# Attention and feed-forward in one kernel: the weighed values of a block accumulate in one PSUM bank, with V scaled by 16

## The reference, cut to what matters

```python
q = einsum('bsd,dhk->bshk', x, Wq) + bq          # k and v likewise
scores = einsum('bqhk,bshk->bhqs', q, k) / sqrt(K)
attn = softmax(scores, axis=-1)
ctx = einsum('bhqs,bshk->bqhk', attn, v)         # the change is here
attn_out = einsum('bqhk,hkd->bqd', ctx, Wo) + bo
```

## Time and profile before

| | |
|---|---|
| median of 3 executions | 3343.22 us (3339.74 to 3346.07) |
| the profiled execution | 3347.19 us, of which the span of the profile is 3345.4 us |
| PE busy | 3095.9 us, 93% of the span, 25440 matmuls |
| DVE busy | 2784.4 us, 83% |
| ACT busy | 2473.8 us, 74% |
| POOL busy | 2016.6 us, 60% |
| mean granted clock of PE | 0.969 of full speed |

### The profile page before, as it was taken

One profiled execution on the slowest core, in us unless ns is written; L12 is line 12 of the kernel. 1 busy time (PEld: TensorE's weight loads), 2 busy tenths in 40 slices (PEclk: granted clock), 3 DMA queues, 4 the chain that ended last, 5 costly groups with the idle time before them and its releaser, 6 DMA issues. The chain is left out here.

```text
span 3345.4 us, 77779 instructions
## 1 busy us (share of the span) xinstructions
PE 3095.9 (93%) x25440; PEld 2475.0 (74%) x25440; DVE 2784.4 (83%) x4983; ACT 2473.8 (74%) x4715; POOL 2016.6 (60%) x1550
## 2 busy tenths in 40 slices
PE   5899999999999999969999999999999999878897
PEld 4677777777777777757777777777777778667775
DVE  5688988888888888976888888888888889578886
ACT  3688888888888788856888787878888889733222
POOL 3577767676667666636777666766667677512232
PEclk9999999999999999989999999999999999989998
DMA  3522222222222122115122222222222222221110
GB/s 106 136 53 53 54 54 54 54 54 54 54 48 57 43 55 56 42 31 172 33 56 57 42 56 46 54 54 54 54 54 54 54 53 52 96 83 51 63 44 19
DMA packets 206585, 197.39 MB, mean 59 GB/s; under 512 B 157648, under 2 KB 180304, under 8 KB 193872
## 3 DMA queue, kind: packets, MB, share of 16 engines
q1 hardware_dynamic: 206160, 192.00, 24.7%
HBM read 53.16 MB, written 37.88 MB: 27 GB/s over the span
## 5 line engine op out<-in xcount | busy, mean ns | idle before, releaser
L442 POOL TENSOR_TENSOR p_l<-p_f,p_h 128x512 f16<-128x512 f32 x1280 | 1627.0, 1293 | 546.9 <-ACT p_h L514 546.1
L562 DVE TENSOR_REDUCE mx<-ps_aux 128x1 f32<-128x512 f32 x2048 | 1384.5, 684 | 289.3 <-PE ps_aux L735 258.8
L513 ACT ACTIVATE p_f<-ps_score 128x512 f32<-128x512 f32 x2048 | 1272.2, 622 | 358.7 <-PE ps_score L746 337.3
L514 ACT ACTIVATE p_h<-ps_score 128x512 f16<-128x512 f32 x2048 | 1283.0, 628 | 0.0
L735 PE MATMUL ps_aux<-k_hihi,q_hilo 128*128 128x512 f32 x2048 | 1037.5, 507 | 93.8 <-DVE mx L562 44.4
L768 PE MATMUL ps_ctx<-v_hi_one_lo,p_h 128*128 128x129 f16 x8192 | 929.2, 223 | 2.3 <-POOL p_l L442 1.5
L768 PEld LDWEIGHTS ps_ctx<-v_hi_one_lo,p_h 128*128 128x128 f16 x8192 | 609.2, 99 | 322.2 <-issue 264.2
L746 PE MATMUL ps_score<-q_hi_max,k_lo_one 65*128 65x512 f32 x2048 | 826.5, 404 | 0.0
L745 PE MATMUL ps_score<-q_hilo,k_hihi 128*128 128x512 f32 x2048 | 821.2, 401 | 3.7 <-DMA q_hi_max<-negm 3.1
L768 PE MATMUL ps_ctx<-v_hi_one_lo,p_l 128*128 128x65 f16 x8192 | 783.3, 195 | 0.0
L735 PEld LDWEIGHTS ps_aux<-k_hihi,q_hilo 128*128 128x128 f32 x2048 | 632.3, 309 | 173.1 <-DVE mx L562 69.1
(11 more groups left out here) (122 smaller groups left out, 2538.4 us busy)
## 6 DMA issues: line engine op xcount, KB each, us to landing
k_hihi<-hi_st SPq DMA_DIRECT2D x64, 512.0 KB, 8.6
v_heads<-v_new SPq DMA_DIRECT2D x64, 258.0 KB, 2.0
v_hi_one_lo<-v_heads SPq DMA_DIRECT2D x32, 516.0 KB, 9.7
q_hilo<-hi_st SPq DMA_DIRECT2D x32, 512.0 KB, 4.4
q_hilo<-lo_st SPq DMA_DIRECT2D x32, 512.0 KB, 6.6
q_hi_max<-hi_st SPq DMA_DIRECT2D x32, 512.0 KB, 9.2
k_lo_one<-lo_st SPq DMA_DIRECT2D x32, 512.0 KB, 10.1
heads<-ctx_n SPq DMA_DIRECT2D x128, 128.0 KB, 2.0
```

Source lines behind the costliest of these rows:

```text
L442: nc.gpsimd.tensor_tensor(p_l[:, r], p_f[:, r], p_h[:, r], ALU.subtract).then_inc(lo_pool, 1)
L513: nc.scalar.activation(p_f[:, r], ps_score[:, bank], ACT.Exp, scale=K ** -0.5)
L514: nc.scalar.activation(p_h[:, r], ps_score[:, bank], ACT.Exp, scale=K ** -0.5).then_inc(exp_done, 1)
L562: nc.vector.reduce_max(mx[:, blk % 2, tt, ch:ch + 1], ps_aux[:, bank], AX_X).then_inc(max_read, 1)
```

## The change

The context of a block accumulates in one bank: 4 x 65 columns instead of 4 x 129. For this the low part of V isn't scaled by 2048 any more; all of V is scaled by 16 instead (the column of ones holds 16 too), so the factor cancels in the division. `p_h` times the 64 low columns now goes onto the same 64 sums as `p_h` times the high ones, which takes a matmul of its own: 12 matmuls a step, of 65, 64 and 65 columns, where there were 8 of 129 and 65. The two banks hold two blocks in turn. ACT's copy and DVE's addition are gone. DVE takes the reciprocal and the product straight from the bank, both in step 4 of the next block. In the prologue DVE scales the bias of V once a batch, and the addition of that bias multiplies by 16 too.

```diff
-LO_SCALE = 2048.0
-SUMS_AT = 4
+V_SCALE = 16.0
+DIVIDE_AT = 4
...
-            def copy_sums(nb):
-
-                act.wait_ge(pv_done, (nb + 1) * KT + PROBS)
-                act.wait_ge(ev_step, nb * 2 + 2)
-                nc.scalar.activation(sums[:, :, :], ps_ctx[:, :, 0:2 * VW], ACT.Copy).then_inc(ctx_free, 1)
...
-                    nc.scalar.activation(v_new[:, k % 4, :, K + 1:VW], vf, ACT.Copy, scale=LO_SCALE)\
-                        .then_inc(v_ready, 1)
+                    nc.scalar.activation(v_new[:, k % 4, :, K + 1:VW], vf, ACT.Copy).then_inc(v_ready, 1)
...
-                    if t % KT == SUMS_AT and not (first and u == 0 and t < KT):
-                        copy_sums((g + u) * NB + t // KT - 1)
...
-            dve.sem_inc(ev_step, 2)
+            dve.sem_inc(ctx_free, 2)
...
-            def add_sums(nb):
-
-                dve.wait_ge(ctx_free, nb + 2)
-                acc = sums[:, :, :].rearrange("p a (t c) -> p (a t) c", c=VW)
-                nc.vector.scalar_tensor_tensor(out=ctx_u[:, :, :], in0=acc[:, :, K + 1:VW], scalar=1.0 / LO_SCALE,
-                                               in1=acc[:, :, 0:K], op0=ALU.mult, op1=ALU.add).then_inc(ev_step, 1)
+            def divide(j, nb):
+
+                acc = ps_ctx[:, j % 2, 0:TB * (K + 1)].rearrange("p (t c) -> p t c", c=K + 1)
+                dve.wait_ge(pv_done, (nb + 1) * KT + PROBS)
                 nc.vector.reciprocal(rden[:, :], acc[:, :, K]).then_inc(ev_step, 1)
-
-            def divide(j, nb):
-
-                dve.wait_ge(ev_step, nb * 2 + 4)
+                dve.wait_ge(ev_step, nb + 1)
                 dve.wait_ge(ctx_out[j % 2], (nb - j) * 8 + j // 2 * 16 + 16)
-                nc.vector.tensor_tensor(ctx_n[:, j % 2], ctx_u[:, :, :],
+                nc.vector.tensor_tensor(ctx_n[:, j % 2], acc[:, :, 0:K],
                                         rden[:, :].unsqueeze(2).to_broadcast([P, TB, K]), ALU.mult)\
-                    .then_inc(ctx_ready, 1)
+                    .then_inc(ctx_free, 1)
...
+                    nc.vector.tensor_scalar(bv_all, bv_all, V_SCALE, None, ALU.mult).then_inc(bv_scaled, 1)
+                    dve.wait_ge(bv_scaled, b + 1)
...
-                    if kt == 2 and block_before:
-                        add_sums((g + u) * NB + j - 1)
-                    if kt == 4 and block_before:
+                    if kt == DIVIDE_AT and block_before:
                         divide((j - 1) % NB, (g + u) * NB + j - 1)
...
                 for q in range(TB):
-                    acc = ps_ctx[:, q // 2, (q % 2) * VW:(q % 2 + 1) * VW]
-                    parts = [(p_h, VW), (p_l, K + 1)]
-                    if q % 2:
-                        parts.reverse()
-                    for p, width in parts:
-                        mm = nc.tensor.matmul(acc[:, 0:width], p[:, r, q * P:(q + 1) * P], V[u][:, kt, 0:width],
-                                              start=(kt == 0 and q % 2 == 0 and p is p_h),
-                                              stop=(kt == KT - 1 and q % 2 == 1 and p is p_h),
-                                              skip_group_check=True)
+                    acc = ps_ctx[:, j % 2, q * (K + 1):(q + 1) * (K + 1)]
+                    toks = slice(q * P, (q + 1) * P)
+                    v_one, v_lo = V[u][:, kt, 0:K + 1], V[u][:, kt, K + 1:VW]
+                    nc.tensor.matmul(acc, p_h[:, r, toks], v_one, start=(kt == 0 and q == 0), stop=False,
+                                     skip_group_check=True)
+                    nc.tensor.matmul(acc[:, 0:K], p_h[:, r, toks], v_lo, start=False, stop=False,
+                                     skip_group_check=True)
+                    mm = nc.tensor.matmul(acc, p_l[:, r, toks], v_one, start=False,
+                                          stop=(kt == KT - 1 and q == TB - 1), skip_group_check=True)
                 mm.then_inc(pv_done, 1)
```

More of the change, by code:

```diff
@@ L171, in attention @@
         negm = sb("negm", [P, 2, TB], F32R)
-        sums = sb("sums", [P, 2, 2 * VW], F32)
         rden = sb("rden", [P, TB], F32)
-        ctx_u = sb("ctx_u", [P, TB, K], F32)
         ctx_n = sb("ctx_n", [P, 2, TB, K], F32)
@@ L520, in head @@
                             .then_inc(xh_ready, 1)
-                    if t % KT == SUMS_AT and not (first and u == 0 and t < KT):
-                        copy_sums((g + u) * NB + t // KT - 1)
-                if last and u == 1:
-                    copy_sums((g + u) * NB + NB - 1)
                 return n
```

13 lines of the change are left out of this document (6 added, 7 removed).

## The result

The changed kernel takes 3384.27 us (median of 4, 3382.91 to 3385.39) against 3344.38 us of the kernel before: a ratio of 1.0122 (1.0109 to 1.0135), so 40 us or 1.2% slower. The forecast was 20 us slower, 3363 us in a range of 3315 to 3425. The profiled execution took 3384.6 us with a span of 3382.7 us, at the same mean granted clock as before, 0.969. So the 39.9 us are work or waits and not the clock.

A forecast was written before the change was run, and what follows sets the result against it. PE's own issue was taken as the bound within a head. Terms +29 (matmuls), +32 (burst end), -42 (DVE's relief) and +1 (ends) gave +20: 3367 us profiled, 3363 us median, with an 8-in-10 range of 3315 to 3425.

The forecast's parts named there:

- PE's two terms: PE's longer stream: the matmuls of a weigh, +29 us, and the end of the burst, +32 us.
- The matmuls of a weigh: PE, each quarter: three short matmuls at 30.5 ns, 91.5 ns against 88, over 8192 quarters: +29 us.
- the end of the burst: PE, last matmul of a burst: 65 columns hide 28 ns less of the next load, 1136 bursts: +32 us.
- The product from PSUM: DVE's product with its first operand in PSUM: 407 ns, its least, in place of a mean of 710.
- The waits that move: DVE's reciprocal now waits for the block's last weigh, with at least 2.3 us of slack: costed at nothing.
- ACT's copy: ACT loses 128 copies of 614 ns and 44.8 us of waiting; not the bound, so worth nothing.
- DVE's relief: DVE saves 1.08 us a block at best, cutting PE's waits for maxima: -42 us, bounds 0 and -55.
- The waits should fall from 44.4 to under 10: PE's waits of maximum tiles for DVE, in us, as a sign that would show the forecast.
- Short matmuls are dear: Rival: adding onto sums just written costs 5 ns more; 3429 us, or 3380 if half pay; set at 3405; chance 0.22.
- The relief wins: Rival: short matmuls at 29 ns or less, DVE gives back 50 us: -26, 3317 us; chance 0.28.
- point of decision: Where DVE's relief exceeds PE's two terms: a short matmul of 30.1 ns at 51 us of relief.
- The change doesn't do what it says: Rival: product from PSUM takes 0.7 us, PE gets back half: +21 more, 3384 us; within the dear side's 0.22.

The follow-up runs named there:

- the first experiment: Kernel before with the parts of a weigh never turned round, p_h first and p_l last, so bursts end with 65 columns: 3359.12 us, ratio 1.0044.

## Why the prediction was half right

The sign and PE's two terms held. The relief of DVE did not: its mechanism was wrong for this order of PE, and its term was nearly twice too large.

*The matmuls of a weigh, +29, and the end of the burst, +32.* Right, and a little low. A burst was to become 56 ns longer (8 quarters of 3.5 ns, and 28 at its end), 2.35 us for two steps; it became 62 ns longer, 2.362 us. That the sums agree so well, 61 forecast and 61.4 in the table, is partly luck: the table has 990 distances and the forecast more bursts. The short matmul was taken at 30.5 ns; from start to start it is 29, 33 and 29 ns in the median behind the three kinds, and 31.2 in the mean of a burst (718 ns in 23 distances). The end of the burst alone is 26 ns of the 28 forecast (the first experiment). That the load starts with the last matmul and takes 0.46 us whatever streams under it is what the earlier trace rows had said.

*The product from PSUM.* Right: 425 ns where 407 was forecast, with a spread of 3 ns where it had been 407 to 1316. "SBUF — State Buffer" of the Trainium skill, section "Who interferes with whom", says that one SBUF input keeps clear of GpSimd, and these numbers agree. The same trace has the other side of it in the subtractions with two SBUF inputs, at 1.54 and 1.24 us beside POOL's.

*The waits that move, and ACT's copy.* Right at nothing. The reciprocal waits for nobody in the timeline above, and for PE in 2 of 128 cases over the trace (4.8 us). ACT's 51 us show nowhere in PE's waits while PE's order is as it was; no run took ACT's copy away alone.

*DVE's relief, -42.* Wrong: the irregular distances gave back 23.6 us, of which 16.5 come with a longer PE stream alone, and the relief was -8 to -22 where it was measured by itself. This is the failing step, in its own sentence: "With 1.08 us less in that stretch most of the lag should be gone: 1.25 - 1.08, about 0.2 us, stay." The 1.08 us are about what was saved (0.78 of the addition, and 0.29 of the product by its mean). But I took DVE's lateness at `w_l` for a debt that runs through from the block's addition, and it isn't one. That "the next maxima run without a pause up to 672.71" was a misreading: DVE was ready and waiting for the tile at 664.88, behind the addition, so the addition's time was paid back before the lag began. In the trace after it stands idle for 0.97 us before 674.03 and is late again at 681.91. The lag is made in the 6 us behind that point, by two subtractions that run slowly beside POOL's, the cast and `w_l`. The earlier trace rows ended in just these, but the rows of the subtractions between 665.48 and 671.51 were left out of the reading, and so was the question that decides it, whether DVE is idle anywhere between the saved work and the late one. Of the saved work only the product's lies behind that point, 1.02 us that became 0.42; against it stand the reciprocal and the wait for it, 0.17 us each, so about 0.25 us is left (1.28 became 1.03), and from the next tile on it hardly shows. The experiments put it where it belongs: with the old order of PE no relief of the block touches the wait (28 times in each), and `w_l` off DVE removes it and is worth 38 to 43 us.

The same error sits in "The waits should fall from 44.4 to under 10": they fell to 36.2, and do so too with DVE untouched.

*The loop's turn.* Not in the sum: 33.6 to 39.4 us, +6. It is the same in the kernel with three matmuls and the old DVE work (39.6), and 34.9 and 32.1 us in the two kernels with eight matmuls a weigh (parts never reversed; DVE relieved), so it comes with PE's instructions. The page shows 4.90 MB of instructions in place of 3.82. That the fetch is what the turn waits for is an inference from these two rows, and no run took it apart.

Those 6 us are among the distances over 0.8 us, whose total falls by 1.7 in spite of them. Put right, the sum for the spans is 61 - 24 - 1 + 1 = 37, with the turn inside the 24; by the medians it is 40.

*The rivals.* "Short matmuls are dear" is out by its price: the same burst with and without a second matmul on the same sums takes 718 and 720 ns. It had stood at 3380 to 3429 us and the time fell into that stretch for another reason, a relief that was not there. A time in the range of a case is no proof of the case. "The relief wins" had its point of decision right (a short matmul of 30.1 ns with 51 us of relief), and missed on both sides of it: 31.2 ns, and 24 us. "The change doesn't do what it says" named 3384 us, the time that came, through a product of 0.7 us. The product took 0.425, so its time was met and its mechanism was not.

## What to carry to other kernels

A lag of an engine can only be paid back by work saved between its last idle moment and the wait. In the trace of before, look for the last operation ahead of the late one that starts as soon as its input is there (a merged row can hide the pause), and count only what the change removes behind it. Splitting a matmul so that two engines that aren't the bound save 1 us of work a block costs the bound engine at its own price at once; here that was 61 us, against 24 us less of waiting. When a wait stands at the same place once in every head, the instruction that stands just before it on the late engine is the first to move. What a relief is worth holds for one order of the other engines: the same change cost 40 us with a maximum tile first and 13 with a score tile first.

## What the runs showed that was not expected

- The order of two tiles behind a burst is worth 0.12 us each time: 466 ns from the last short matmul to the second start with a maximum tile first, 345 ns with a score tile first. It gave 38 us in the kernel before and 66 in the changed one. The maximum tile is one matmul with a load of 0.31 us; the score tile's first start comes 0.02 us after the burst (1002.07 to 1002.09).
- Three short matmuls, each with its load, stand 29, 33 and 29 ns apart, 24 in a row in 718 ns. The second and the third add onto sums that the one before has just added to; with the second in columns of its own the burst takes 720 ns, so this costs nothing that can be seen.
- A wait of PE of 1.9 us from start to start (249.82 to 251.70) can be followed by a stretch at half the clock (251.90 to 255.30 us at 0.50), and then costs more than its own length: a maximum tile and the burst behind it took 1.90 us there, where they took 0.92 at the full clock.
- A slower PE stream eats a part of its own cost: +26 ns a burst gave 15 us in place of 26, since the waits for DVE shrink with it.
- The same subtraction of 512 numbers on DVE takes 1.24 to 1.54 us beside POOL's, and the maxima of 512 numbers out of PSUM stay at 0.68 us throughout.
